# The counts of a block's turn first, an extra turn amid a tile's last group, and clears of one column

## What is computed

```python
src, dst = (edge_index[0], edge_index[1])
h = jnp.concatenate([x, node_emb[node_type]], axis=-1)
h = jax.nn.relu(rgcn_conv(h, src, dst, edge_type, W1, root1, b1))   # sums by (dst, type), by 1/count, times W[type]
h = jax.nn.relu(rgcn_conv(h, src, dst, edge_type, W2, root2, b2))
h = rgcn_conv(h, src, dst, edge_type, W3, root3, b3)
...
msgs = edge_e[:, None] * h[dst]                        # layer 1: a function of the edge's two ends
h_prime = jax.ops.segment_sum(msgs, src, num_segments=n)
...
msgs = edge_weight[:, None] * x[row]                   # layer 2
agg = jax.ops.segment_sum(msgs, col, num_segments=x.shape[0])
...
summed = jax.ops.segment_sum(edge_attr, col, num_segments=n)   # layer 3
```

## Time and profile before

| | |
|---|---|
| median of 3 runs | 5415.35 us (5401.39 to 5419.33) |
| the profiled execution | 5398.16 us, its span 5396.4 us |
| PE busy in the span | 3765.6 us (70%) |
| PEld, DVE, ACT, POOL busy | 56%, 49%, 22%, 44% |
| mean granted clock of PE | 0.794 |

### The profile page before, as it was taken

The page is one execution under the profiler, slowest core; times in us unless marked ns, Lnnn a source line. Parts: engine busy times, 40 slices in busy tenths (PEclk is TensorE's granted clock), DMA queues, the critical chain, the costliest instruction groups (busy, mean ns, idle before and its releaser), DMA issues.

```text
span 5396.4 us, 103191 instructions
## 1 busy us (share of the span) xinstructions
PE 3765.6 (70%) x20688; PEld 3046.7 (56%) x20691; DVE 2663.4 (49%) x6964; ACT 1163.5 (22%) x3868; POOL 2356.5 (44%) x2346
## 2 busy tenths in 40 slices
PE   4777677788888766666666776767676766757873
PEld 1333566666666655555555555656565655656762
DVE  7654454444444455545544544444444444892235
ACT  0122111121222111111222222222222222441112
POOL 0000465555555454545555555556555553003430
PEclk8999788888889877766766667887777776888886
DMA  2022333444444322222222223333333432436640
GB/s 73 32 66 75 103 108 114 117 120 118 119 126 133 110 55 55 55 58 64 76 76 74 77 82 104 109 109 108 104 105 107 111 107 67 170 134 176 179 118 12
DMA packets 478385, 526.90 MB, mean 98 GB/s; under 512 B 96596, under 2 KB 398238, under 8 KB 474670
## 3 DMA queue, kind: packets, MB, share of 16 engines
q1 hardware_dynamic: 252780, 246.52, 14.7%
q0 software_dynamic: 85824, 199.51, 13.8%
q10 hardware_dynamic: 139746, 80.46, 5.1%
HBM read 399.82 MB, written 126.39 MB: 98 GB/s over the span
## 4 chain that ended last, share of the span: by engine, by line
PE 31%; issue 25%; DMA 9%; DVE 9%; another core or an unknown queue 7%; POOL 6%; ACTq 4%; ACT 3%; DVEq 3%; SPq 2%; POOLq 1%
DMA msg_r<-y_tab,idx_r 7%; PE psum L1616 6%; POOL msg_r L635 6%; PE psum L1894 3%; PE psum L1689 2%; PE psum L1618 2%; PE psum L1804 1%; DVE shot_r L1151 1%; PE psum L1765 1%; PE psum L1805 1%; DVE h_t L1413 1%; ACT idx_r L712 1%; PE psum L1554 1%; PE psum L1542 1%
## 5 line engine op out<-in xcount | busy, mean ns | idle before, releaser
L635 POOL DMA_INDIRECT msg_r<-y_tab,idx_r x2160 | 2198.1, 1018 | 2327.9 <-issue 1115.5
L1616 PE MATMUL psum<-shot_r 128*128 128x200 f32 x2604 | 982.1, 478 | 404.8 <-issue 207.7
L1145 DVE SCALAR_TENSOR_TENSOR shot_r<-edge_f,win_base,iota 128x600 bf16<-128x600 f32 x434 | 366.3, 844 | 1437.3 <-remote 849.4
L712 ACT COPY idx_r<-row_i 128x1 int32 x2142 | 396.0, 191 | 1921.3 <-DMA msg_r<-y_tab,idx_r 1092.7
L1616 PEld LDWEIGHTS psum<-shot_r 128*128 128x128 f32 x2604 | 542.0, 258 | 438.4 <-issue 433.6
L1689 PE MATMUL psum<-hot_r,msg_r 128*128 128x128 f32 x2880 | 510.4, 320 | 162.1 <-DMA msg_r<-y_tab,idx_r 134.9
L1804 PE MATMUL psum<-msg_r,shot_r 128*128 128x128 f32 x1440 | 394.1, 364 | 305.4 <-DMA msg_r<-in_attr 103.7
L1689 PEld LDWEIGHTS psum<-hot_r,msg_r 128*128 128x128 f32 x2880 | 420.8, 219 | 231.4 <-DMA msg_r<-y_tab,idx_r 143.7
L1131 DVE TENSOR_SCALAR hot_r<-iota,edge_g 128x128 f32<-128x128 f32 x1602 | 446.4, 354 | 181.4 <-PE psum L1805 90.3
L1618 PEld LDWEIGHTS psum<-shot_r 128*100 128x100 bf16 x2604 | 430.2, 165 | 128.6 <-issue 20.3
L1804 PEld LDWEIGHTS psum<-msg_r,shot_r 128*128 128x128 f32 x1440 | 279.1, 241 | 375.2 <-issue 183.2
(11 more groups left out here) (315 smaller groups left out, 4746.5 us busy)
## 6 DMA issues: line engine op xcount, KB each, us to landing
msg_r<-in_attr SPq DMA_DIRECT2D x882, 64.0 KB
h_t<-count_tab SPq DMA_DIRECT2D x25, 1600.0 KB, 6.7
w_tab<-shot_r ACTq DMA_DIRECT2D x385, 100.0 KB
count_tab<-shot_r ACTq DMA_DIRECT2D x385, 100.0 KB
h_t<-w_tab SPq DMA_DIRECT2D x24, 1600.0 KB
msg_r<-y_tab,idx_r POOLq DMA_INDIRECT x2160
xn<-heavy_tab SPq DMA_DIRECT2D x76, 320.0 KB
y_tab<-y_s SPq DMA_DIRECT2D x25, 640.0 KB, 2.9
```

Of the source, the lines that this page charges most:

```text
L635: pool.indirect_dma_start(out=msg_r[:, q, 0:width], out_offset=None, in_=table, in_offset=bass.IndirectOffsetOnAxis(ap=idx_r[:, q:q + 1], ...
L712: nc.scalar.copy(idx_r[:, q:q + 1], of[:, q:q + COLS - U + 1][:, bass.ds(c0, 1)]).then_inc(s_idx[k], 1)
L1145: V.scalar_tensor_tensor(out=key_b, in0=of(KEY, KW), scalar=win_base[:, bass.ds(w, 1)], in1=to(KW), op0=ALU.subtract, op1=ALU.is_equal).th ...
L1616: T.matmul(win_ps, low_f[:, i, :], weighted_f[:, i, :], start=False, stop=False)
```

## The change

It has three parts.

1. DVE makes key_b and low_b first, and low_b raises s_key_hot; then low_f, behind s_seen, and weighted_f. PE waits for s_key_hot, makes the six count matmuls of the visit and raises a new semaphore, s_counted; then it waits for s_see, makes the three weight sums and raises s_seen. DVE's key_b waits for s_counted and for its own s_see, and low_f for s_seen.
2. Pass 1's extra turn stands on PE between the sums of the third and fourth chunk of the tile's last group, no longer behind the sixth. DVE's and ACT's order stay.
3. The clears and closes of the prologue's counts (384 columns) and windows (500 columns), and those of a tile's sums in passes 0 and 2 (256 columns), are made on one spare column (LAST_COL, 511) of the same bank. The matmul of zeros over 500 columns at each visit of a prologue window (L1572) stays.

```diff
-                    dve.wait_ge(s_seen, v)
-                    V.scalar_tensor_tensor(out=key_b, in0=of(KEY, KW), scalar=win_base[:, bass.ds(w, 1)], in1=to(KW),
-                                           op0=ALU.subtract, op1=ALU.is_equal).then_inc(s_key_hot, 1)
-                    V.tensor_tensor(out=low_f, in0=to(P), in1=of(LOW, P), op=ALU.is_equal)
-                    V.tensor_tensor(out=low_b, in0=to(P), in1=of(LOW, P), op=ALU.is_equal)
+                    dve.wait_ge(s_counted, v)
+                    dve.wait_ge(s_see, v)
+                    dve.sem_inc(s_go, 1)
+                    V.scalar_tensor_tensor(out=key_b, in0=of(KEY, KW), scalar=win_base[:, bass.ds(w, 1)], in1=to(KW),
+                                           op0=ALU.subtract, op1=ALU.is_equal)
+                    V.tensor_tensor(out=low_b, in0=to(P), in1=of(LOW, P), op=ALU.is_equal).then_inc(s_key_hot, 1)
+                    alone(dve)
+                    dve.wait_ge(s_seen, v)
+                    V.tensor_tensor(out=low_f, in0=to(P), in1=of(LOW, P), op=ALU.is_equal)
                     alone(dve)
                     dve.wait_ge(s_key_hot, v)
                     V.tensor_tensor(out=weighted_f, in0=key_b, in1=of(WGT, KW), op=ALU.mult).then_inc(s_see, 1)
...
-                    pe.wait_ge(s_see, v)
+                    pe.wait_ge(s_key_hot, v)
                     for i in range(VR):
-                        T.matmul(win_ps, low_f[:, i, :], weighted_f[:, i, :], start=False, stop=False)
                         for b in range(2):
                             last = T.matmul(count_ps[:, b, :], key_b[:, i, b * TURN:(b + 1) * TURN], low_b[:, i, :], start=False, stop=False)
+                    last.then_inc(s_counted, 1)
+                    alone(pe)
+                    pe.wait_ge(s_see, pe.snap(v + 1))
+                    for i in range(VR):
+                        last = T.matmul(win_ps, low_f[:, i, :], weighted_f[:, i, :], start=False, stop=False)
                     last.then_inc(s_seen, 1)
...
                 for q in range(U):
+                    if k == 1 and last and q == UH:
+                        window_sums()
+                        pe_blocks.fetch()
                     if q % UH == 0:
...
-            def extra1(D, last):
-                window_sums()
-                pe_blocks.fetch()
-
-            gathering(1, start1, chunk1, stop1, lambda D: table3(D - 1), extra1)
+            gathering(1, start1, chunk1, stop1, lambda D: table3(D - 1))
...
-                    T.matmul(psum[0:U * R, 4 + h, 0:UH * P], zeros_b[:, 0:U * R], zeros_b[:, 0:UH * P], start=True, stop=False)
+                    T.matmul(psum[0:U * R, 4 + h, LAST_COL:LAST_COL + 1], zeros_b[:, 0:U * R], zeros_b[:, 0:1], start=True, stop=False)
...
-                    clear(window)
+                    spare = psum[:, bass.ds(pe.snap(w % 2 * 4 + 3), 1), LAST_COL:LAST_COL + 1].rearrange("p o n -> p (o n)")
+                    clear(spare)
...
-                    close(window, s_win)
+                    close(spare, s_win)
...
-                clear(acc0(slot, 0, 2))
+                clear(spare0(slot))
...
-                close(acc0(slot, 0, 2), s_sums[0])
+                close(spare0(slot), s_sums[0])
```

More of the change, by code:

```diff
@@ L40 @@
 TURNED, SPARE = 264, 240
+LAST_COL = 511
 TURN = KW // 2
@@ L244, in build @@
         s_y_free, s_y_out = [sem("s_y_free0"), sem("s_y_free1")], [sem("s_y_out0"), sem("s_y_out1")]
-        s_key_hot, s_see, s_seen, s_wsum, s_wgone = [
-            sem(f"s_{n}") for n in ("key_hot", "see", "seen", "wsum", "wgone")]
+        s_key_hot, s_see, s_seen, s_counted, s_wsum, s_wgone = [
+            sem(f"s_{n}") for n in ("key_hot", "see", "seen", "counted", "wsum", "wgone")]
         s_w_out, s_ct_out, s_agg_o, s_agg_out = [sem(f"s_{n}") for n in ("w_out", "ct_out", "agg_o", "agg_out")]
@@ L587, in _ @@
             pool.sem_inc(s_seen, 1)
+            pool.sem_inc(s_counted, 1)
+            pool.sem_inc(s_see, 1)
             pool.sem_inc(s_w_out, 16)
@@ L1559, in first_table @@
                 for h in range(2):
-                    last = T.matmul(psum[0:U * R, 4 + h, 0:UH * P], zeros_b[:, 0:U * R], zeros_b[:, 0:UH * P],
+                    last = T.matmul(psum[0:U * R, 4 + h, LAST_COL:LAST_COL + 1], zeros_b[:, 0:U * R], zeros_b[:, 0:1],
                                     start=False, stop=True)
@@ L1673, in acc0, with spare0 @@
                 return psum[:, bass.ds(slot, 1), m * P:(m + n) * P].rearrange("p o f -> p (o f)")
+            def spare0(slot):
+                return psum[:, bass.ds(slot, 1), LAST_COL:LAST_COL + 1].rearrange("p o f -> p (o f)")
             def start0(D, slot):
                 pe.wait_ge(s_inv_in, D)
-                clear(acc0(slot, 0, 2))
+                clear(spare0(slot))
                 root0(D, lambda m: acc0(slot, m))
@@ L1807, in stop2 @@
             def stop2(slot):
-                close(acc0(slot, 0, 2), s_sums[2])
+                close(spare0(slot), s_sums[2])
             pe.wait_ge(s_y_ev[1], TILES + 1)
```

## The result

The changed kernel takes 5323.72 us (median of 4 runs, 5305.94 to 5337.4), the kernel before, with one more run beside it, 5417.34 us (5401.39 to 5443.7). The ratio is 0.9847 (95% interval 0.9808 to 0.9886): faster, but by 83 us (by the ratio) to 94 us (by the medians) and not by the 169 that were forecast. 5246 us was predicted; the measured time lies in the range of 5170 to 5385, in part by luck, as the parts show.

A forecast was written before the change was run, and what follows sets the result against it. Pass 1 was taken as 130 us longer than its gathers ask for, PE and DVE handing one buffer to and fro, and PE as the prologue's bound; -75 -10 -60 -22 -7 +5 = -169 us gave 5246 us, range 5170 to 5385.

The forecast's parts named there:

- The extra turn amid the group: Pass 1's tile boundaries: the extra turn runs while PE waits for messages, 2.5 us saved per tile, -60 us (0 to -110).
- The counts first: DVE and PE turns: counts precede sums and free the next key hot early; -75 double, -10 single turns, +5 added waits.
- double turns: Pass 1's 49 turns with a second visit: its key and low hots overlap the first visit's sums, -75 us (-40 to -98).
- single ones: Turns with one visit, all passes: counts leave the tail, but mostly gathers end the group; -10 us (0 to -40).
- the floor of 9.64 us: POOL's cadence in pass 2: a group of six gathers cannot be much shorter while releases come as there.
- Passes 0 and 2: Turns mostly hide behind gathers: part of -10 us for single turns, -7 for clears; each changes by under 30 us.
- Rival A: PE's releases come late whatever PE does, so shorter turns lengthen waits: -65 us, 5350 us; chance 0.28 together with Rival D.
- The prologue: One-column clears and closes replace 384 and 500 columns; PE is the bound, so nearly all counts: -22 us (-8 to -36).
- rival C: TensorE's clock: prologue falls to 0.86, 5275 us; or pass 1 rises to 0.78, 5200 us (0.12, shared with upper bounds).
- The passes' clears: Passes 0 and 2, tile boundaries: 96 clears of 256 columns cut to one column, -7 us (0 to -15).
- Rival B: Pass 1: PE stalls at the extra turn, chunk buffers stay taken, gathers run late; 5450 us, chance 0.10 with other stalls.
- Rival D: DVE's key finds s_counted as late as s_seen was; doubles give only -20, 5301 us; chance 0.28 together with Rival A.

## Why the prediction was right in its sign and wrong in its size

**The extra turn amid the group (-60): right where releases are timely.** 62 and 56 us alone; on a chip with late ones it was not run alone. What it named as the mechanism is in the rows: the turn under the wait for messages, the last sum not followed by it.

**The counts first (-75 for double turns, -10 for single ones, +5 for waits): mechanism right, a term mis-sized where releases are timely.** There it is 165 to 186 us in place of 80. Second visits overlap as worked out, 3.79 us from sums to sums in the row above with a slow-clock visit in it, and 3.3 was said. The step that failed there is "in the single turns of pass 1 the counts leave the tail too (0.34 to 0.64 us), but what ends the group is mostly the gathers". The last 60 groups of pass 1 gained 0.7 us each; the rows above draw a visit's six counts with 0.51 us at the fast clock and 0.85 at the slow one. Over 120 groups that is 84 us where I had some part of 10. If the first 60 groups gained the same 0.7 us by their single turns, the remainder, (1.6 - 0.7) x 60 = 54 us, is what their 47 second visits gave, an estimate of 1.1 us each and not 1.5. The view that should have told it is the earlier trace rows: 85 waits of PE for the weighted hot are more than the 49 double turns can have. Also the floor of 9.64 us was one of late releases: where they are timely, the last 60 groups of the changed kernel's pass 1 take 8.6 us each. On a chip with late releases the small term may have been about right, since there the order alone gave the last 60 groups some 0.1 us each.

**Passes 0 and 2 (-10 and -7, asked to "keep 9.7 us of cadence and change by under 30 us each"): wrong on this chip.** They grew by 29 and 52 us in the profiles (10.9 and 11.0 us a group). The step that failed is the assumption that a turn which ends earlier can at worst change nothing in them. Rival A, the late release, is nearer in number, 5350 us against my 5246 for a measured 5324, and late releases are there in plenty; I had the rows for them (4.2 us in the earlier trace rows, 3.0 of them with ACT idle) and took the timely handovers of one double turn for the rule. But A is not right in its place either: it let pass 1 gain only some 45 us (35 and 10) and had no growth anywhere, and pass 1 gained 157 while passes 0 and 2 lost 81. In the changed kernel the chunk sums' releases are late by over 0.5 us in 936 of 1373 cases within gathers (766 of 1240 before). In pass 2 POOL's wait for PE's chunk sums rose; in the changed kernel it is

```profile
POOL msg_r L638 <- PE psum L1819: 382.8, 113, 9.8
```

and in the kernel before

```profile
POOL msg_r L635 <- PE psum L1805: 279.8, 91, 9.8
```

Where late releases don't occur, the same kernel gains 184 to 192 us, so half of the gain goes with the condition of the chip. That it is the lateness itself, and not something that comes with it, is the likeliest reading and not shown. Why a chip has late releases, and why passes 0 and 2 grew, stays open: no part of the change but the order without its signal and the prologue's clears ran on such a chip, and the order alone does not make more releases late (848 of 2160 above). Of the 29 and 52 us a part may also be scatter, since the passes of one kernel differ by 10 to 20 us between profiles.

**The prologue (-22): wrong, and rival C in its first form was right.** The first gather came 29 us later, not 22 earlier. The failed step is "PE is the bound in the prologue, so nearly all counts": the 30.8 us of saved busy time were there, but at the price of the clock. I gave C a fall to 0.86; it fell to 0.77. Whenever the windows' matmuls of zeros were cut, the clock fell and the time rose. With the counts' alone the clock fell to 0.83 and the time did not change by anything that can be told (1.0008).

**The passes' clears (-7): nothing to be measured,** 1.0009.

**Rival B,** a stall that holds up the gathers, did not come: alone, the extra turn gains in every run. **Rival D** neither, as the row at 1787.53 shows.

**The sum.** With timely releases: -166 counts first, -62 extra turn, +24 prologue, +3 passes' clears are -201, and -192 and -184 were measured, so the parts add up within 17 us. In the first measurement the forecast's -169 became -61 between the two profiled executions and -83 to -94 over all runs. By the profiles the prologue is 51 us worse than said and passes 0 and 2 some 95 worse, while pass 1 (-157 in place of about -135) and the rest are better. That the time lies within the range is luck in this respect: the misses of the prologue and of passes 0 and 2 come to some 146 us, nearly as much as the whole forecast, and the range, drawn for other reasons, was wide enough for them.

## What to carry to other kernels

A matmul that computes nothing can be worth its time: before clearing by one column in a stage that TensorE bounds, read the stage's granted clock, and try the edit by itself. If two engines hand a buffer to and fro, let the part that is ready first go first, on a signal of its own (what the signal adds to the order was not measured by itself where releases are timely), and count the gain in all turns where one waits for the other, not only in those with a second visit. Before a gain is summed up, look in the trace for releases that reach the waiting engine long after the work has ended; where they are, time saved on the releasing engine may not come through; the same program was 9 to 10% slower on one chip than on another.

## What the runs showed of the hardware

- The kernel before takes 4907 to 4913 us in four groups on three chips and 5330 and 5417 us in two other measurements. In the passes with gathers, the semaphore of a chunk sum changes over 0.5 us after the sum's modelled end in 951 of 2160 cases on the first chip, in 14 of 2160 on a timely one. DVE's releases are late as well, and 540 register operations take over 0.5 us on the first chip, none on the timely one. Prologues, which have no gathers, take the same (first gather at 546 and 549 us).
- Cutting 191 matmuls of zeros from 500 columns to one made the prologue some 50 us longer, at a granted clock of 0.70 in place of 0.92 or 0.93; both levels, 1.2 and 2.4 GHz, occur in it, and the mean says how much of each.
- The clear by one column takes 163 to 194 ns on average in the changed prologue (clock 0.77), against 331 to 422 ns for one of 384 or 500 columns in the prologue of before (0.93).
